# First attention: the second group of transposes at the end of a slot

## The reference

```python
x = x + _L0_attn_ref(_layernorm(x, axis=-1), Wq, Wk, Wv, Wo, bo)
...
q = (x @ Wq).reshape(b, n, H, DH)          # H = 16 heads, DH = 64
k = (x @ Wk).reshape(b, n, H, DH)
v = (x @ Wv).reshape(b, n, H, DH)
scores = jnp.einsum('bihd,bjhd->bhij', q, k) * scale + bias[None]
scores = jnp.where(causal[None, None], scores, jnp.float32(-1e+30))
attn = jax.nn.softmax(scores, axis=-1)
out = jnp.einsum('bhij,bjhd->bihd', attn, v).reshape(b, n, H * DH)
return out @ Wo + bo
```

## Time and profile before

| | us |
|---|---|
| median of three runs | 1681.77 |
| the profiled execution | 1697.44 |
| its span | 1695.0 |
| TensorE busy in the span | 1497.4 (88%) |
| VectorE busy | 1156.6 (68%) |
| ScalarE busy | 1019.2 (60%) |
| GpSimd busy | 477.9 (28%) |

### The profile page before, as it was taken

One profiled execution on the slowest core, in us unless ns is written; L12 is line 12 of the kernel. 1 busy time (PEld: TensorE's weight loads), 2 busy tenths in 40 slices (PEclk: granted clock), 3 DMA queues, 4 the chain that ended last, 5 costly groups with the idle time before them and its releaser, 6 DMA issues. The chain is left out here.

```text
span 1695.0 us, 39542 instructions
## 1 busy us (share of the span) xinstructions
PE 1497.4 (88%) x11574; PEld 1104.9 (65%) x11575; DVE 1156.6 (68%) x3609; ACT 1019.2 (60%) x2667; POOL 477.9 (28%) x732
## 2 busy tenths in 40 slices
PE   6999999999999786789999488888888869887798
PEld 4777777777777564578888355555555535555597
DVE  5776777677777487756666367777777639993465
ACT  5776777777777364656666256666666625553254
POOL 4333333333332244023332222222222012221033
PEclk9999999999999887899999789999999979997999
DMA  6000000000000300011111100000000000000000
GB/s 203 2 0 0 0 0 0 0 0 0 0 0 1 144 31 25 5 37 43 43 43 42 55 13 12 8 12 12 12 11 8 1 1 2 0 0 0 1 26 25
DMA packets 34214, 34.67 MB, mean 20 GB/s; under 512 B 5744, under 2 KB 29936, under 8 KB 33392
## 3 DMA queue, kind: packets, MB, share of 16 engines
q1 hardware_dynamic: 29808, 25.08, 4.6%
q0 software_dynamic: 4352, 8.92, 2.1%
HBM read 25.07 MB, written 8.91 MB: 20 GB/s over the span
## 5 line engine op out<-in xcount | busy, mean ns | idle before, releaser
L596 POOL TENSOR_SCALAR a_prob<-a_prob,a_inv 128x128 f32<-128x128 f32 (+1 forms) x256 | 126.5, 504 | 358.3 <-DVE a_inv L496 358.3
L430 ACT ACTIVATE a_prob<-a_psS,a_low 128x128 f32<-128x128 f32 (+1 forms) x512 | 210.0, 436 | 0.0
L486 DVE CUSTOM_DVE_ANT_0 a_psS<-a_psS,a_bias 128x128 f32<-128x128 f32 (+1 forms) x512 | 167.8, 390 | 44.9 <-PE a_psS L308 31.8
L1753 ACT ACTIVATE a_probT<-a_psZ 128x512 f32<-128x512 f32 x256 | 138.9, 595 | 90.2 <-PE a_psZ L1565 71.5
L1826 DVE TENSOR_REDUCE a_low<-a_psS 128x4 f32<-128x1024 f32 x128 | 156.2, 1221 | 52.9 <-remote 34.5
L421 ACT COPY a_probT<-a_psT 128x384 f32<-128x384 f32 x256 | 123.5, 482 | 94.9 <-PE a_psT L352 93.7
L352 PE MATMUL a_psT<-ident,a_prob 128*128 128x128 f32 x768 | 138.7, 290 | 2.9 <-ACT a_probT L421 2.8
L1311 POOL DMA_INDIRECT d_rows<-rows_dram,source x72 | 67.9, 943 | 194.7 <-PE e_psX L1393 143.3
L308 PE MATMUL a_psS<-a_qk 64*128 64x128 f32 (+1 forms) x1024 | 119.8, 353 | 1.7 <-ACT a_qk L413 0.7
L352 PEld LDWEIGHTS a_psT<-ident,a_prob 128*128 128x128 f32 x768 | 80.1, 140 | 54.3 <-issue 46.5
L430 ACT ACTIVATION_READ_ACCUMULATOR a_prob<-a_psS,a_low 128x1 f32 x512 | 113.4, 221 | 0.0
(11 more groups left out here) (329 smaller groups left out, 4161.4 us busy)
## 6 DMA issues: line engine op xcount, KB each, us to landing
sorted_out<-e_y SPq DMA_DIRECT2D x72, 64.0 KB, 1.5
in_lo<-in_gate_up SPq DMA_DIRECT2D x4, 1024.0 KB, 7.9
x<-in_x SPq DMA_DIRECT2D x8, 256.0 KB, 6.8
down<-in_down SPq DMA_DIRECT2D x1, 2048.0 KB, 15.0
rows_dram<-rows SPq DMA_DIRECT2D x8, 256.0 KB, 2.3
out<-x SPq DMA_DIRECT2D x8, 256.0 KB, 2.3
d_rows<-rows_dram,source POOLq DMA_INDIRECT x72
a_sel_in<-in_sel SPq DMA_DIRECT2D x1, 1024.0 KB
```

What stands on the lines that cost most here:

```text
L430: nc.scalar.activation(prob[:, 2 * (p % 4) + k, lo:hi], psS[:, u, lo:hi], ACT.Exp, bias=low[:, u, i:i + 1], scale=-1.0, accum_out=total[:, ...
L486: nc.vector.tensor_tensor_reduce(psS[:, u, lo:hi], psS[:, u, lo:hi], bias0[:, 2 * p + k, lo:hi], 1.0, LEAST, ALU.add, ALU.min, low[:, u, i ...
L596: nc.gpsimd.tensor_scalar(w, w, inv[:, 2 * (q % 2) + 1, i:i + 1], 1.0, ALU.mult, ALU.mult).then_inc(norm_done[1], 1)
L1753: nc.scalar.activation(probT[:, (p + half + 1) % 2, 2 * half + c, :, :].rearrange("p j s -> p (j s)"), psZ[:, c, :], ACT.Exp, scale=-1.0). ...
```

## The change

In TensorE's slot, `turn(b, p, 1)` moves behind `values_in` and `values`. It stays ahead of what slots 3, 5 and 7 have at their end. No instruction of another engine moves, and no buffer changes.

```diff
@@ -384,12 +384,12 @@
                         project(b, p + 1)
                     elif prep and p == PAIRS - 1:
                         project(b + 1, 0)
-                    if has_unit(p, 2):
-                        turn(b, p, 1)
                     if new:
                         values_in(b, p, prep, has_unit)
                     if has_unit(p, 3):
                         values(b, p)
+                    if has_unit(p, 2):
+                        turn(b, p, 1)
                     if p == 3 and has_unit(p, 8):
                         tail_of_batch_before(b, p, new)
                     if p == 5 and prep:
```

## The result

The changed kernel takes 1704.38 us (median of four runs, 1702.08 to 1706.98), the kernel before 1681.51 in the runs beside it. The ratio is 1.0134, with a 95% interval of 1.0120 to 1.0149: 22.9 us slower, where +14.4 was forecast. The sign and the places of the loss were right, the sizes of two terms were not. The time lies 0.4 us above the range (1687 to 1704).

What follows compares the result with a forecast made beforehand. TensorE was taken to set the pace, busy 33.56 of 34.18 us per batch. Slot terms of 0.96 us per batch over 15 edges gave +14.4 us on a median of 1681.77: 1696 us, range 1687 to 1704.

Steps and rivals of the forecast that it cites:

- The ordinary slot: TensorE saves 0.42 us between the projections and pays 0.48 at the slot's end: +0.06, to 3.67 us.
- The rule of weight loads: Loads run beside a matmul only in another row group; by it the ordinary slot would come out at 0, not +0.06.
- Slots 4 and 5: The block moves into TensorE's wait for VectorE's copy of v: 0 gained, 0 lost, together 8.2 us.
- printed wait in slot 5: Sign at slot 5's end: TensorE's 0.56 us wait for v's copy should shrink to under 0.3.
- Slot 3: Ends in 32 full-array output matmuls, so no change of array is added: taken as 0, between -0.06 and +0.06.
- Slot 6: The next batch's norm copy on ScalarE still precedes v's projection, by 0.3 us; only the ordinary +0.06.
- the worse edge: Rival: slot 6's 0.3 us of cover fails, +0.6 us more on 15 batches, +9, 1705 us; chance 0.10.
- Slot 0: TensorE waits 0.46 us for ScalarE's late cur_hi before v's projection: +0.52 with the ordinary 0.06; wait bounds 0 to 1.0.
- Slot 7: ScalarE's late rounding delays VectorE's subtraction and the q/k projection from 1.30 to 1.50 us: +0.20, and the ordinary +0.06.
- The sum: Slots 1, 2 and 6 0.18, slot 7 0.26, slot 0 0.52: 0.96 us per batch, 14.4 us over 15 edges.
- TensorE's price alone: Rival: ScalarE's delay is absorbed at the edge, leaving 0.2 to 0.3 us per batch, +4, 1685 us; chance 0.12.
- Faster: Rival: slot 5's wait absorbs the block, v's copy comes earlier and ScalarE keeps up: 1679 us or less; chance 0.04.

Runs made afterwards that it cites:

- e5_round: Changed kernel, but ScalarE rounds the next batch's input (slot 6) ahead of the copy of the second transposes: 1693.84 us, 1.0079 to the kernel before.
- e7_both: Changed kernel with ScalarE's rounding and its copy of the input for v both moved ahead of the second transposes' copy: 1685.97 us, 1.0019 to the kernel before.
- e11_v5: Kernel before, with VectorE's copy of v in slot 5 ahead of the reciprocal and the scaling of the probabilities: 1687.93 us, 1.0036.
- e9_mid_both: e8_mid plus ScalarE's earlier rounding and copy for v, the norm's copy ahead of slot 7's exponentials: 1685.36 us, 1.0016 to the kernel before.
- e8_mid: Kernel before, with the second transposes moved between the projection of v and the values: 1676.61 us, 0.9966.

## Why the prediction was half right

**The ordinary slot: right.** +0.06 forecast, +0.07 to 0.08 measured, by the named distances. The rule of weight loads from the Trainium skill, "TensorE: Matmul & The Clock Gate", section "The mechanism", would have given 0, and the slot speaks against it. The same section also excepts loads into a background weight buffer, which the prediction left out; with that exception the rule says nothing against this trace.

**Slots 4 and 5: right in the sum.** 8.20 before and after; only the printed wait in slot 5 shrank less than forecast. **Slot 3:** taken at 0, it is -0.11: the block takes 0.38 to the output (242.45 to 242.83 in the trace), full array behind full array, and the output's 32 matmuls take 3.67 us to the next scores instead of 3.77. My bounds of 0.06 were too narrow. **Slot 6:** the cover of the norm's copy held (the copy ends at 256.40, v's projection starts at 256.65), and so the worse edge (1705) did not occur, though the time came out near it by another way.

**Slot 0: right place, a mis-sized term.** "Slot 0: +0.46 + 0.06 = +0.52" measured +0.77 to +0.82. The block started where it was put, but the norm's transposes and the loop's edge behind it took 0.38 to the scores instead of 0.50, and the first group 0.39 (forecast 0.38). Slot 0 thus began 0.11 earlier and TensorE waited that much longer for a copy that did not come earlier. Another 0.07 us of the wait are signals and lengths on ScalarE: the projection started 3.36 behind the block, forecast 3.29. So the wait was 0.63 instead of 0.46. The last 0.10 is the slower step behind a wait from v's first matmul to its second, for which the sum had no term.

**Slot 7: the step that failed, again by its size.** "Slot 7: +0.20, and the ordinary +0.06" measured +0.47 to +0.52, although the edge gave back 0.12. In the projection's start it was +0.20 forecast, +0.51 measured. The term is "0.06 for the signal, an estimate from the steps of 0.03 and 0.13": the signal from ScalarE's rounding to VectorE's subtraction takes 0.24 us. And the length: 0.42 in rows 5, where the queue was full, 0.50 behind this wait. These two are 0.26 of the 0.31 us, and the other 0.05 are the rounding's: it ended at 0.94 instead of 0.89. e5_round, which takes this path away, brings back all of it.

**The sum.** As means over the loop, slots 0 and 7 are +1.26 (0.78 forecast), 1, 2 and 6 +0.23 (0.18), 3 -0.11 (0), 4 and 5 0: 1.37 us per batch from edge to edge instead of 0.96, times the 14 batches of the loop 19 us; the two batches that are written out differ by 2.0 us from the second profile of the kernel before (34.04 + 30.36 against 32.56 + 29.85). In the first of them the first slots vary by over 1 us from run to run of one order (slots 0 and 1 take 9.15 and 10.27 in the two profiles of the kernel before), so of that I can call only the last batch's 0.5 the change's, and 0.8 in slots 6 and 7 of the first (4.13 and 4.11 against 3.74 and 3.73). The two edge terms were 0.48 us too small, which over 15 edges is 7 of the 8.5 us missed.

**The range.** It ended at 1704 because I gave the waits a third of error in a forecast of 1696 and left the rest to one rival. The upper bound that I had written for slot 0's wait alone, 1.0 us instead of 0.46, is worth 15 x 0.54 = 8 us and leads from 1696 to 1704 by itself. So the range had no room for an error in slot 7 beside one in slot 0, and both came.

**The rivals.** TensorE's price alone is what e7_both measures (1686), only not what the change does. "Faster" rested on v's copy coming earlier: in the changed kernel v was done at 252.66 and its copy started at 253.78, out of VectorE's queue, and slots 4 and 5 kept their 8.20. In e11_v5, where the copy does come earlier, the kernel is slower.

## What to carry to other kernels

When a block is moved to a later place on the busiest engine, price it by the starts around it at both places, and then follow what the engine that drains it does next in its own order: here 0.5 us too late for a rounding and 0.6 for a copy, on an engine with a quarter of its time idle, made four fifths of the loss. Putting one instruction ahead in another engine's order removes the wait for it and delays all behind it: in e11_v5 a reciprocal 0.33 us late came back as a batch 0.34 longer, over a third engine. And a wait that is only predicted is a sum of small steps (signal, length, the way from one place to another), taken here from rows in which little or nothing waited. Most of them came out longer once something did wait, and the edge was priced 40% too low; such a sum needs a range of its own.

## What the runs showed of the hardware

- Three 128x128 transposes cost TensorE 0.34 us between full-array matmuls and values, 0.42 between two full-array projections and 0.48 between two half-array blocks. In the 0.42 there is, as an estimate, 0.02 of waiting for the bank, since the block started 0.05 us behind the end of the copy in most slots of the kernel before.
- From the end of an instruction on ScalarE to the start of the VectorE instruction that waited for it 0.24 us passed in the loop, against 0.05 from ScalarE to TensorE (265.56 to 265.61). In the first batch, which is written out, the same pair took 0.14 (46.42 to 46.56). What the loop adds was not tried.
- The same VectorE subtraction took 0.42 us behind another instruction and 0.50 behind a wait in the loop. In the first batch it took 0.42 behind a wait of 1.02 us too, so a wait alone does not lengthen it.
- The second attention took 384.8 us from its first projection to its last product with v in one execution, and 370.3 to 370.5 in all 13 other profiles; the granted clock in the windows of the result, 0.98 and 0.97, does not explain it. The cause is open.
- TensorE idle for 2.29 us at the end of the last batch of e9_mid_both was followed by a granted clock of 0.51 for 6 us; the same work in e8_mid, with waits up to 1.11 us, kept 1.00. That the idle time is the cause was not tried.
